# Products with a matrix of zeros in the waits of TensorE: the last stage of a decoder layer

## The reference

```
x = x + delta_attention(layernorm(x))          # 16 key heads, 32 value heads of 128
x = x + cross_attention(layernorm(x), ctx)     # 32 query heads of 8, 8 key/value heads, 64 context rows
h = gelu(layernorm(x) @ w1q.T + b1)            # w1q, w2q: ternary weights, 1024 hidden values
x = x + (h @ w2q.T + b2)
```

## Time and profile before

| | us |
|---|---|
| median of 3 runs | 2584.98 (2584.34 to 2587.34) |
| the profiled execution, own time | 2580.95 |
| its span in the profile | 2579.1 |
| last stage: from VectorE's last sum of the second stage to the end | 2019.7 to 2579.1 |

### The profile page before, as it was taken

How to read it: one execution, slowest core, us unless ns; L and a number is a source line. 1 busy time by engine, 2 the same in 40 slices (tenths; PEclk the granted TensorE clock), 3 DMA queues, 4 the chain that set the end, 5 groups by cost and what they waited for, 6 DMA issues and landing times.

```text
span 2579.1 us, 64198 instructions
## 1 busy us (share of the span) xinstructions
PE 2218.8 (86%) x22592; PEld 1422.6 (55%) x22592; DVE 1841.7 (71%) x2925; ACT 1477.5 (57%) x2755; POOL 1088.6 (42%) x1439
## 2 busy tenths in 40 slices
PE   2486689999999999999999999999888688778787
PEld 2232245656655565565555556566555466666665
DVE  7775577877878887787778878878555545655655
ACT  3475556666666666666666666666555344544544
POOL 1016484572845638356283653836620111212222
PEclk9998889999999999999999999999999658878878
DMA  7446523243242333324324233342421101100100
GB/s 292 143 116 134 132 73 83 78 97 85 71 99 79 83 90 88 87 68 92 95 68 95 88 79 84 96 89 63 97 57 39 53 13 30 30 27 29 29 14 18
DMA packets 500783, 205.23 MB, mean 80 GB/s; under 512 B 437072, under 2 KB 454224, under 8 KB 498512
## 3 DMA queue, kind: packets, MB, share of 16 engines
q1 hardware_dynamic: 500432, 200.76, 30.7%
HBM read 128.33 MB, written 72.35 MB: 78 GB/s over the span
## 4 chain that ended last, share of the span: by engine, by line
PE 56%; issue 13%; SPq 8%; ACT 8%; DVE 8%; DMA 4%; POOL 2%; ACTq 0%; POOLq 0%; DVEq 0%
PE PS L1270 16%; PE PS L1284 10%; PE PS L1348 7%; PE PS L1456 3%; PE PS L1437 3%; PE PS L1470 3%; PE PS L1364 3%; DVE Y L1020 3%; ACT XN L788 3%; PE PS L1321 2%; PE PS L1498 2%; ACT Y L769 2%; SPq L377 1%; DMA SCR<-PGD 1%; SPq L431 1%
## 5 line engine op out<-in xcount | busy, mean ns | idle before, releaser
L1020 DVE SCALAR_TENSOR_TENSOR Y<-PS,CW,Y 128x504 f32<-128x504 f32 (+2 forms) x1536 | 1115.3, 732 | 442.5 <-ACT Y L762 389.9
L762 ACT ACTIVATE Y<-PS,CW 128x512 f32<-128x512 f32 x512 | 398.1, 777 | 466.4 <-PE PS L1270 454.8
L1284 PE MATMUL PS<-WOS,XN 128*128 128x256 f16 x3072 | 378.2, 273 | 2.2 <-DVE XN L1035 1.1
L1284 PEld LDWEIGHTS PS<-WOS,XN 128*128 128x128 f16 x3072 | 300.9, 98 | 92.9 <-issue 2.1
L626 POOL TENSOR_TENSOR SQ<-KQ 128x512 f32<-128x512 f32 x128 | 137.6, 1075 | 461.8 <-PE PS L1312 370.3
L1270 PE MATMUL PS<-XK,WH 128*128 128x512 f16 x1024 | 312.6, 387 | 16.3 <-DMA XK<-XHD 16.3
L1270 PE MATMUL PS<-XV,WH 128*128 128x512 f16 x1024 | 307.5, 382 | 8.4 <-issue 7.8
L612 POOL TENSOR_TENSOR SCR<-SCR 128x31 f32<-128x31 f32 (+15 forms) x496 | 291.2, 587 | 38.9
L1348 PE MATMUL PS<-XN,M 64*64 64x256 f32 x2048 | 248.9, 381 | 48.9 <-ACT XN L788 48.0
L609 POOL TENSOR_TENSOR SCR<-SCR 128x31 f32<-128x31 f32 (+15 forms) x496 | 260.3, 525 | 33.0
L788 ACT ACTIVATE XN<-PS,KN 128x256 f32<-128x256 f32 x512 | 212.6, 466 | 62.6 <-PE PS L1284 62.5
(11 more groups left out here) (138 smaller groups left out, 3152.3 us busy)
## 6 DMA issues: line engine op xcount, KB each, us to landing
PGD<-SCR SPq DMA_DIRECT2D x128, 256.0 KB, 2.1
SCR<-PGD SPq DMA_DIRECT2D x128, 256.0 KB, 3.1
EQD<-XN SPq DMA_DIRECT2D x32, 512.0 KB, 4.1
SCR<-EQD SPq DMA_DIRECT2D x128, 128.0 KB, 2.6
SCR<-QND SPq DMA_DIRECT2D x128, 128.0 KB, 3.3
XP<-in_x SPq DMA_DIRECT2D x16, 512.0 KB, 4.6
SCR<-in_wall SPq DMA_DIRECT2D x8, 1024.0 KB, 7.1
SCR<-PGD SPq DMA_DIRECT2D x64, 128.0 KB, 3.0
```

Of the source, the lines that this page charges most:

```text
L762: A_.activation(Y[:, b, :], PJ[b][:, :], ACT.Identity, scale=CW[:, h[1] % NH, cw0 + 3:cw0 + 4], bias=CW[:, h[1] % NH, cw0 + 4:cw0 + 5]).th ...
L1020: V_.scalar_tensor_tensor(yv[:, :, m:T], pv[:, :, 0:T - m], CW[:, h[1] % NH, cw0 + 3 - m:cw0 + 4 - m], yv[:, :, m:T], ALU.mult, ALU.add).t ...
L1284: ins = mm(VWB[:, E * i:E * i + E], VHL[:, vk, n, P * a:P * a + P], WOS[:, wk, 2 * (w[1] % NH) + n, :], start=(t == 0), stop=(t == 5))
```

## The change

TensorE gets additional products whose moving operand is zero, at fixed places of its order in the last stage. One such product has the f16 identity as weights, 256 columns of zeros as moving operand, and adds to the first 256 columns of a bank. The zeros are the first 128 f32 columns of `SQ`, read as f16; GpSimd clears `SQ` once, ahead of the stage. All are issued unconditionally: TensorE does not look whether it would wait.

- Before the stage's first transposes: 130 products into bank 2, and 6 more behind the transposes. Bank 2 is one of the banks of `scores`, which later writes it anew.
- In groups 0 to 7, in u = 1, 2, 3, 5, 6, 7: products into bank 7 at three places: 5 at the start of the step, 4 ahead of `scores` (10 in u = 3 and 7), and 4 ahead of `transposes_of` (12 in u = 1 and 5).
- In u = 1 and 5, TensorE first waits until VectorE has read bank 7 (`x3_done`).

```
+            idle = SQ[:, 0:P].bitcast(F16)
+            def keep_busy(n, bank=F2B):
+                for _ in range(n):
+                    mm(bank[:, 0:E], IDH[:, :], idle, start=False, stop=True, skip_group_check=True)
+            pe.wait_ge(S["idle_zero"], 1)
+            keep_busy(130, BANK[2])
             rows_transposed(0)
+            keep_busy(6, BANK[2])
             scores(0, 0)
...
                 for u in range(8):
+                    fill = live and u not in (0, 4)
+                    if fill and u in (1, 5) and i:
+                        pe.wait_ge(S["x3_done"], at(2 * i - 2 + u // 4))
+                    if fill:
+                        keep_busy(5)
                     if u == 0 and last:
                         weighted(i - 1, 3)
                     if u in (2, 4, 6) and live:
                         weighted(i, u // 2 - 1)
+                    if fill:
+                        keep_busy(10 if u in (3, 7) else 4)
                     if u < 6 and live:
                         scores(i, u + 2)
...
+                    if fill:
+                        keep_busy(12 if u in (1, 5) else 4)
                     if live:
                         transposes_of(i, u)
```

More of the change, by code:

```diff
@@ L194, in build @@
         HT = GT // 2
-        names = "ld_const ld_w0 ld_w1 ld_w2 ld_w3 ld_tern ld_tern2 w_split w_hi tern_sum tern_all tern_done zeroed conv_scaled".split()
+        names = "ld_const ld_w0 ld_w1 ld_w2 ld_w3 ld_tern ld_tern2 w_split w_hi tern_sum tern_all tern_done zeroed conv_scaled idle_zero".split()
         owned = {
@@ L655, in _ @@
                 v = VBS[n]
+                if n == 0:
+                    nc.gpsimd.memset(SQ[:, :], 0.0).then_inc(S["idle_zero"], 1)
                 nc.gpsimd.memset(v[:, :, :, :], 0.0).then_inc(S["zeroed"], 1)
```

## The result

The kernel with the change takes 2520.49 us in the median of 4 runs (2513.26 to 2523.12), the kernel before 2586.16 (4 runs): a ratio of 0.9741, 95% interval 0.9728 to 0.9754, 65.7 us less.

A forecast was written before the change was run, and what follows sets the result against it. TensorE's own time, stretched by its falling clock, was taken as the bound. Gains of 2.3, 15.7, 39 and 13.5 us sum to 70.5, giving 2510.5 profiled and 2514.5 median; the 8 in 10 range was 2496 to 2562.

The forecast's parts named there:

- TensorE's own time sets the pace, and it is the clock that stretches it: Last stage, steady groups: TensorE busy 262 of 326.5 us; steps at the low clock cost nearly twice as much.
- An empty wait of about 1.9 us brings the clock down: Waits in u = 5 and u = 1: the clock falls just behind them and rises only when `summed` begins.
- Price of a product 0.109 us, unhidden 3.7 us a group: Added products at the high clock: 0.109 us apiece; those in no wait cost 3.7 us of a steady group.
- Sum: Whole last stage: 2.3 + 15.7 + 39 + 13.5 = 70.5 us gained.
- the start: Stage start to group 0's `rows_transposed`: 130 products take 14.2 us, so it starts 2.5 us late.
- group 0: Group 0 to group 1's `rows_transposed`: 34.9 us instead of 39.7, with one clock fall in u = 0.
- each steady group: Five groups from 2142.1 to 2468.6: each takes 57.5 us instead of 65.3, 7.8 less.
- group 1's first part: From group 1's `rows_transposed` to the next group's: 55.3 us instead of 71.0, 15.7 gained.
- the end: Behind 2468.59, from u = 6 of group 6 on: 13.5 us gained, "group 8" unchanged.
- The bound of what was not seen: Added products with zeros: they count for the clock like `summed` or not at all; the first was taken.
- the second rival's mechanism: Transposes in u = 5 and 6 don't count as busy, so the clock falls once a group: 2558 us, chance 0.12.
- x3_done: New TensorE waits in u = 1 and 5: should end at once, as VectorE adds the sum a whole step before.

The follow-up runs named there:

- e1: The change with only the 136 products at the start of the stage, none inside the groups: 2586.79 us, ratio 1.0010 to the kernel before.
- e7: On e3, only the 15 products in u = 3 and 7 of groups 1 to 7 left: 2563.92 us, ratio 0.9915 to the kernel before.
- e3: The change, keeping in groups 1 to 7 only products that lie in a TensorE wait: 2493.42 us, ratio 0.9656 to the kernel before.
- e6: On e3, only the 12 products in u = 1 and 5 of groups 1 to 7 left: 2525.36 us, ratio 0.9771 to the kernel before.
- e5: The change without its 21 products in u = 1 and 5 of groups 1 to 7: 2539.78 us, ratio 0.9819 to the kernel before.
- the second profile of the change: The change, unedited, measured again with more rounds: 2514.17 us, ratio 0.9728 to the kernel before; last stage 489.5 us.
- e4: On e3, 10 f32 transposes replace the 12 products in u = 1 and 5 of groups 1 to 7: 2499.40 us, ratio 0.9671.
- e2: The change with zeros as weights and dense W1 columns moving, same 984 products: 2511.46 us, ratio 0.9727 to the kernel before.
- e8: On e3, 106 products at the start instead of 130, 24 in group 0's first long wait, otherwise only u = 7's 15 there: 2482.60 us, ratio 0.9614.

## Why the prediction was right

- *TensorE's own time sets the pace, and it is the clock that stretches it.* Shown: 37.6 us less over five groups (326.5 to 288.9) although 58 us of products were added, `weighted` 2.05, and e1, in which everything but the products inside the groups is as in the change and the gain is nought.
- *An empty wait of about 1.9 us brings the clock down.* Shown for u = 1 and 5 by e7 against e3 (10.3 us a group), for the longer ones of u = 3 and 7 by e6 (3.9, with the 5 products of u = 2). But the length of the wait is not the rule that the prediction made of it. Before the change the clock fell behind all 14 waits of 1.9 us and in only 5 of the 14 of 2.73 us; in e5 it fell behind 9 of 14 of 1.9 us; and it fell behind 0.74 us and less in the second profile of the change, e4 and e6. What TensorE does around the wait counts with it: e5 and e7 leave the same 14 waits empty and differ in the products elsewhere. That 1.1 us was the longest wait left in a steady group was thus no proof that the clock would hold, though in both profiles it did.
- *Price of a product 0.109 us, unhidden 3.7 us a group.* 130 took 14.35 with the tail of the last; 9 took 1.08 up to the next step, where 0.98 was charged. Without the products in no wait a group was 3.4 shorter (e3).
- *Sum.* 69.9 us in the last stage (559.4 - 489.5) against 70.5. The terms that were off: the start took 0.5 more, since the first product came 0.47 us behind VectorE's sum; group 0 took 1.4 less; each steady group cost 0.26 more, 1.3 in all, and group 1's first part 0.7; the end took 0.4 less. Group 0 is in part luck: its 33.5 us are those of the first profile, where the clock stood at 0.50 for 3.4 us. The seven other profiles with the same group 0 have 34.8 to 35.1, with 34.9 forecast, and there it stood at 0.50 for 6.8 us, or fell a second time. The second profile of the change came to the same 489.5 by another way, 1.6 more in group 0 and 1.7 less at the end, where the fall in "group 8" was missing. That VectorE's wait would shrink by 5 us was read too high: it shrank by 3.1 in u = 3 and 4.0 in u = 7.
- *The bound of what was not seen.* I took it that zeros count. e2 shows that neither operand's zeros matter. So it is hardly for their zeros that `scores` and `weighted` leave a low clock low. Whether it is for their columns or their rows was not tried.
- *The Trainium skill's rule on transposes*, the second rival's mechanism, did not decide: no fall in u = 5 or 6 in either profile of the change, and e4 (above) held the clock with f32 transposes.
- *x3_done.* No wait for it, as forecast: VectorE's sum of line 1173 starts at 2205.89 and at 2235.73, and the products that need it start at 2213.83 and 2241.95, over 6 us later. For the 984 products the line's view names only the start of the stage and TensorE's own issue.

```profile
  issue: 19.9, 47
  DVE XP L1054: 1.8, 1
```

Left open: why the clock falls more often in the second stage of some executions than of others, whether these falls explain all of its 10 us, and exactly where the edge lies between small products that hold the clock and those that let it fall (u = 4 in e4; group 0 in the second profile of the change).

## What to carry to other kernels

Where an in-order TensorE waits some 2 us at fixed points and the profile shows its clock at 0.50 for many us behind them, full-array products with zeros inside these waits are worth a try: here they were worth far more than they cost. Put about as many there as the wait holds, and none elsewhere: that gave 34 us beyond the change. Fill all long waits or expect the next one to take over: of the 10.9 us a group that both kinds gave, one alone gave 7.0, the other 0.6. Look at more than one profile, since the edge is near: the same code held the clock in one execution and lost it in another. And read the stage that was edited by its own length, since the rest of the kernel may scatter by more than the terms that are argued over.

## What the runs showed of the hardware that was not expected

- The clock is held by less than it takes to raise it. In e1 it stood at 0.50 for 60.8 us in which TensorE was busy 53.9 with `scores`, transposes and `weighted`; in e8 the same kinds of step, entered at 1.00, kept it for 27 us. It isn't safe there: among the same steps it fell in u = 4 of group 0 in three profiles, the second one of the change, e4 and e6.
- The longer of two empty waits was the safer one: before the change the clock fell behind 14 of 14 waits of 1.9 us and in 5 of 14 of 2.73 us. Behind the long one the next f16 products start 2.0 us after its end (2221.14 to 2223.09), behind the short one 9.4 us (2236.75 to 2246.14). That this is the reason is not shown by itself.
- Ten f32 transposes of the identity held the clock through all 14 waits of 1.9 us, as 12 f16 products do (e4, e3).
